# Second cross attention: VectorE copies the values and splits the context between the transposes of the second image's probabilities

## What is computed

```python
q = _split_heads(query @ Wq + bq)
k = _split_heads(key @ Wk + bk)
v = _split_heads(value @ Wv + bv)
score = jnp.einsum('bhqd,bhkd->bhqk', q, k) / scale
score = score + mask * -1000000000.0
attn = jax.nn.softmax(score, axis=-1)
ctx = jnp.einsum('bhqk,bhkd->bhqd', attn, v)
ctx = ctx.transpose(0, 2, 1, 3).reshape(query.shape[0], -1, D)
return ctx @ Wo + bo
```

## Time and profile before

| | us |
|---|---|
| median of 3 runs | 1159.03 |
| lowest and highest | 1158.91, 1160.18 |
| the profiled execution | 1158.4 |
| its span (first to last instruction) | 1157.1 |
| TensorE busy | 1134.1 |
| VectorE busy | 749.6 |
| ScalarE busy | 537.0 |
| GpSimd busy | 244.7 |

### The profile page before, as it was taken

One profiled execution on the slowest core, in us unless ns is written; L12 is line 12 of the kernel. 1 busy time (PEld: TensorE's weight loads), 2 busy tenths in 40 slices (PEclk: granted clock), 3 DMA queues, 4 the chain that ended last, 5 costly groups with the idle time before them and its releaser, 6 DMA issues.

```text
span 1157.1 us, 21749 instructions
## 1 busy us (share of the span) xinstructions
PE 1134.1 (98%) x8729; PEld 845.8 (73%) x8729; DVE 749.6 (65%) x1523; ACT 537.0 (46%) x1036; POOL 244.7 (21%) x308
## 2 busy tenths in 40 slices
PE   7999999999999999999999999999999999999997
PEld 4655488776658777777777777777888678887886
DVE  6367488769894756666566666665797866546632
ACT  3244457653222655656565656555554532223421
POOL 2300013266740432121212222211431100000000
PEclk9999999999999999999999999999999999999999
DMA  9759710100305264444444445444800502224211
GB/s 349 275 216 395 282 51 1 49 35 1 109 19 182 44 139 93 92 92 92 92 92 92 94 91 101 91 102 76 115 13 2 81 3 35 37 38 75 35 37 36
DMA packets 325671, 111.57 MB, mean 96 GB/s; under 512 B 301834, under 2 KB 302908, under 8 KB 321348
## 3 DMA queue, kind: packets, MB, share of 16 engines
q1 hardware_dynamic: 324224, 109.11, 37.3%
q10 hardware_dynamic: 1348, 1.09, 0.3%
HBM read 65.59 MB, written 20.97 MB: 75 GB/s over the span
## 4 chain that ended last, share of the span: by engine, by line
PE 90%; DVE 5%; SPq 2%; DMA 1%; issue 1%; ACT 1%; POOL 0%; DVEq 0%; ACTq 0%
PE bank L303 66%; PE bank L1972 3%; PE bank L583 2%; PE bank L601 2%; PE bank L1988 2%; PE bank L1163 2%; PE bank L259 2%; SPq L1871 2%; PE bank L519 1%; PE bank L1185 1%; PE bank L1130 1%; PE bank L1127 1%; PE bank L1114 1%; PE bank L2445 1%; DVE stats L227 1%
## 5 line engine op out<-in xcount | busy, mean ns | idle before, releaser
L1909 POOL COPY PT<-W 32x512 f32<-32x512 f32 x120 | 84.0, 700 | 308.4 <-DVE W L2122 227.2
L2111 DVE CUSTOM_DVE_ANT_0 W<-bank,W 128x512 f32<-128x512 f32 x128 | 80.8, 687 | 102.0 <-PE bank L1972 98.5
L2202 ACT ACTIVATE K<-bank,vecT 128x512 f32<-128x512 f32 x64 | 43.8, 689 | 164.5 <-PE bank L303 164.5
L2223 ACT ACTIVATE W<-W,low 128x512 f32<-128x512 f32 x128 | 90.7, 711 | 16.9 <-DVE low L2111 16.9
L303 PE MATMUL bank<-xT,wT 128*128 128x512 f32 x384 | 92.6, 390 | 0.8 <-ACT W L3161 0.5
L303 PE MATMUL bank<-Wkv,Wq 128*128 128x512 f32 x384 | 92.7, 396 | 0.0
L303 PE MATMUL bank<-Wkv,ctxT 128*128 128x512 f32 x384 | 92.0, 394 | 0.0
L303 PE MATMUL bank<-ctxT,Wkv 128*128 128x512 f32 x384 | 90.1, 392 | 1.2 <-DVE ctxT L320 1.2
L303 PE MATMUL bank<-Wq,Wkv 128*128 128x512 f32 x384 | 89.8, 390 | 0.0
L303 PE MATMUL bank<-woT,hR 128*128 128x512 f32 x384 | 87.8, 390 | 0.7 <-DVE W_late L3073 0.5
L303 PEld LDWEIGHTS bank<-Wkv,ctxT 128*128 128x128 f32 x384 | 70.8, 188 | 22.2 <-ACT K L2202 5.7
(11 more groups left out here) (377 smaller groups left out, 2119.9 us busy)
## 6 DMA issues: line engine op xcount, KB each, us to landing
PT<-W SPq DMA_DIRECT2D x360, 64.0 KB, 2.1
W<-ctx_turned SPq DMA_DIRECT2D x16, 1024.0 KB, 5.8
W<-in_ctx_dram SPq DMA_DIRECT2D x8, 1024.0 KB, 11.2
ctx_turned<-ctxT SPq DMA_DIRECT2D x8, 1024.0 KB, 8.2
ctx_turned<-W SPq DMA_DIRECT2D x8, 1024.0 KB, 7.1
XT<-in_ctx_dram SPq DMA_DIRECT2D x4, 1024.0 KB, 11.6
XT<-in_L_ffn_wi_dram SPq DMA_DIRECT2D x64, 64.0 KB, 2.1
raw_own<-in_ctx_dram SPq DMA_DIRECT2D x3, 1024.0 KB, 11.1
```

The costliest lines, as they stand in the source:

```text
L1909: pool.tensor_copy(there, here).then_inc(kept_p.s, 1)
L2111: dve.tensor_tensor_reduce(out=PR[:, j, :], in0=bank[:, 4 + j % 4, :], in1=mask, scale=1.0, scalar=3.0e38, op0=ALU.add, op1=ALU.min, accum ...
L2202: act.activation(K[:, m, :], bank[:, n % 4, :], ACT.Identity, bias=pcol("L1_xattn_bk", m)).then_inc(ring_a.s, 1)
L2223: act.activation(PR[:, j, :], PR[:, j, :], ACT.Exp, bias=low[:, j:j + 1], scale=-1.0, accum_out=total[:, j:j + 1]).then_inc(expd.s, 1)
```

## The change

It is in `vector` and for image 1 alone (`i == 1`); the other engines keep their order, and no instruction is added or taken away.

- the copy of values 0 moves up, ahead of score rows 4 to 7;
- of the first four transposes two stay where they were; then come the second reciprocals, the copy of values 1, and the four subtractions that split the context of image 2 (`context_v(2, r)`), and behind them the other two transposes (probabilities 2 and 3);
- the attended product's copy and the transposes of probabilities 4 to 7 follow, with no subtractions between them.

```diff
--- before.py
+++ after.py
@@ -2149,18 +2149,24 @@
                     for t in range(4):
                         scores_v(i, t)
                     recips_v(i, 0)
+                    if i == 1:
+                        value_v(1, 0)
                     for t in range(4, XPAIRS):
                         scores_v(i, t)
                     if i == 0:
                         value_v(0, 0)
                     if more:
-                        for t in range(4):
+                        for t in range(2 if i == 1 else 4):
                             probs_v(i, t)
                         recips_v(i, 1)
-                    if i:
-                        value_v(i, 0)
                     if i == 1:
                         value_v(1, 1)
+                        for r in range(4):
+                            context_v(2, r)
+                        for t in (2, 3):
+                            probs_v(1, t)
+                    elif i:
+                        value_v(i, 0)
                     if i:
                         attended_v(i - 1)
                     if not more:
@@ -2168,7 +2174,7 @@
                     if i != 1:
                         value_v(i, 1)
                     if more:
-                        if i:
+                        if i > 1:
                             for r in range(4):
                                 context_v(i + 1, r)
                         for t in range(4, XPAIRS):
```

## The result

| | before | with the change |
|---|---|---|
| median of 6 runs | 1158.98 us | 1162.47 us |
| lowest and highest | 1158.69, 1160.18 | 1161.95, 1165.36 |
| the profiled execution | 1158.4 | 1162.05 |
| its span | 1157.1 | 1160.8 |

The ratio is 1.0033, with a 95% interval from 1.0023 to 1.0043: **slower by 3.5 us**. I had forecast 1161.2 in a range that ended at 1162.4, and given "within 0.2%" the larger share. The time lies just over the range, and next to the rival that I had priced at 1162.9 and given 0.09, the fall of TensorE's clock.

What follows compares the result with a forecast made beforehand. TensorE, 98% busy, was taken to bound the kernel. Strips delayed 3.16 us put image 1's attended product 2.2 us later, the 1.16 us saved included: 1159.03 became 1161.2 us, range 1159.2 to 1162.4.

Steps and rivals of the forecast that it cites:

- within 0.2%: Outcome class: whole time within about 2.3 us of the kernel before, too little to tell from no change; given 0.57.
- the fall of TensorE's clock: Rival: TensorE's clock falls in the new 3.3 us stop before image 1's attended product, costing 1.7 us; 1162.9, chance 0.09.
- the slack of the strips: Image 1's last copied strip lands about a microsecond before its attended product on TensorE needs it.
- VectorE's steps: Reordered VectorE work on images 1 and 2: subtractions start at 413.24, take 2.50 us; probabilities 2 and 3 end 3.16 later.
- the sum: Last strip lands at 433.92 + 3.16 - 0.21 = 436.87, so image 1's attended product starts at 437.1.
- The first term, +2.2 us at the attended product: Late strips start image 1's attended product at 437.1 instead of 434.89; +2.0 to +2.4 by the first dozen's pace.
- The granted clock stays at 1.00: Sign expected in the changed kernel's profile: no drop of TensorE's clock through its 3.3 us stop.
- The rival's price: Clock fall costs 1.7 us: at the kernel's start 16 transposes took 3.65 us, later 1.91; chance 0.09.
- Nothing absorbs the shift: Behind image 1's attended product both orders match and TensorE is busy almost throughout, so the +2.2 us stays.
- The gain that the change reaches for: TensorE's 1.16 us wait for VectorE's subtractions, ahead of the keys of image 2, goes away.
- wait gone, strips in time: Rival: the 1.16 us wait ahead of image 2's keys goes and the strips are not late; 1157.9, chance 0.08.

Runs made afterwards that it cites:

- load_last: Changed kernel, but for image 1 SyncE issues the load of image 3's context behind the second dozen of strips; 1.0009 against the kernel before, median 1159.95 us.
- the change's second trace: Profile of the unaltered changed kernel, run again beside the follow-up runs; that batch measured 1.0035 against the kernel before, median 1162.86 us.
- ahead_2: Changed kernel with two of the four subtractions moved behind probabilities 2 and 3; 1.0024 against the kernel before, median 1162.93 us.
- swap: Changed kernel, but for image 2 too the values 1 product and its copy go ahead of the previous image's attended product; 1.0014 against the kernel before.
- fill: Changed kernel plus twelve extra, unused TensorE matmuls in the stop before image 1's attended product; 1.0024 against the kernel before, median 1161.64 us; repeated, 1.0033.
- four_first: Changed kernel with all four first transposes ahead of the subtractions; 0.9994 against the kernel before, median 1158.53 us.
- best_near: `four_first` plus one wait holding GpSimd's first-half strip copies of image 1 until the subtractions are done; 0.9993 against the kernel before, median 1158.91 us.
- copy_only: Kernel before with only the copy of values (1,0) moved ahead of score rows 4 to 7 of image 1; 1.0000 against the kernel before.

## Why the prediction was wrong

- **What bounds the kernel, and the slack of the strips.** Right. The queue's twenty-four strips were the next thing late, and moving the load off them gives 2.1 us back (`load_last`).
- **VectorE's steps.** Right in size. Without the 0.21 us the reciprocals came at 412.55 (I said 412.53 to 412.67 with the hand-over), the subtractions took 2.50 us as chosen, not 3.33, and the copy by GpSimd starts behind them. One step was missing: I took the casts by ScalarE to be ready at their old time. With the subtractions moved forward the load of that context is on the path (it landed at 413.09, ScalarE waited 0.39 us for it, VectorE 0.25). Probability 3 was ready 3.5 us later, not 3.16. In the change's second trace this wait isn't there, and the sum holds.
- **The first term, +2.2 us at the attended product.** 2.47 and 2.14 in two traces. Right. The first dozen took 8.14 and 8.01 us, where I had taken the middle of 7.98 and 8.40.
- **The step that failed** is that the sum put the fall of TensorE's clock at nothing: "The granted clock stays at 1.00". It fell in the new stop and cost 1.43 us in the profiled execution and 1.61 in the change's second trace, on top of the +2.2. I had described this as a rival and given it 0.09, because I had one row of a stop that brought the clock down, over 4 us, and read it as if shorter ones did not. It bounds nothing from below: stops of 3.90, 3.58, 3.77 and 2.65 us all did, while 1.56 and 1.36 us did not in their traces. The stop was mis-sized as well, 3.90 and 3.58 us for 3.3, but `ahead_2` shows that 3.3 would not have been short enough either. The page of the Trainium skill that I set against it (TensorE: Matmul & The Clock Gate, Why this matters for your kernels), with its advice to leave no idle gap between bursts of matmuls, was the better guide: the traces agree with it from 2.65 us up, and show no fall at 1.56 us and below. Had I given this rival the larger share, the forecast would have been 1162.9.
- **The rival's price** of 1.7 us is near the 1.4 to 1.6 us that three orders of VectorE lost, but in part by luck. I took it from slower transposes at the kernel's start as if their clock had been low. The view gives a clock of 1.00 for that stretch, and no row shows a lower one; the trace's clock records begin only at about 11.7 us, behind the slower transposes. That the clock made those 1.7 us is not shown.

```profile
9.00:10.00 1.00, 1.00 (x6) 1.00 (x5) 0.69 (x1) 0.73 (x2) 0.00 (x0) 1.00 1.05 406
```

- **Nothing absorbs the shift.** Right in the main: 3.80 us at image 4, 3.4 at image 15 (796.80 less 402.13, against 793.21 less 401.92) and 3.7 at the end. That VectorE's lateness "comes no later than TensorE wants it" was right only because TensorE was as late itself; `swap` shows it.
- **The gain that the change reaches for.** I took 1.16 us, the gap. It was 1.50: besides the gap, TensorE went 0.2 us slower into it, and its keys took 11.17 us for 11.04 behind it. The gain was in my sum only as what the stop swallowed, so this changed nothing there, but the rival "wait gone, strips in time" should have been 1157.5.
- **What stays open.** The change's executions spread from 1161.8 to 1165.8 us, and those of the kernel before beside its second batch from 1157.8 to 1161.5. In the change's second batch the clock over the whole span ran from 0.999 (1161.92 us) to 0.995 (1165.82 us), so in some executions the clock may not fall and in some it may stay low longer. Neither of these two was profiled. The one that was, at 1164.20 us and 0.996, shows a single fall of the usual size, so its 2.15 us over the first profile are not a second fall. Nor is it settled how much of the 1.4 us the matmuls of `fill` give back in the whole.

## What to carry to other kernels

A wait on the bounding engine is worth only as much as the slack of the wait behind it: list, for the same stretch, what lands next and how long before it is wanted (here 0.7 us), and leave a queue of small DMAs and whoever feeds it out of what is delayed. If a change makes TensorE stand for some microseconds, count the clock's fall as part of the price unless a stop of about that length is in the trace with the clock at 1.00 through it and behind it. And look at which engine starts at the same signal: here VectorE's subtractions and GpSimd's copies started together. The order within VectorE brought the keys 0.50 us forward (`four_first`), and keeping the two apart 0.87 us more (`best_near`), though neither shows in the whole time before the load is moved too.

## What the runs showed of the hardware that I had not expected

- The clock of TensorE can fall when TensorE is at work again: in `ahead_2` it stood for 2.65 us, went on at 436.30, and the granted clock left 1.00 only within the stretch from 437. In the four traces with a fall the clock was at 0.50 for 3.4 us, and the matmuls took 1.43, 1.61, 1.59 and 1.56 us longer.
- Four subtractions of 128x512 on VectorE take 2.48 to 2.50 us alone, 3.33 where GpSimd's copies begin 1.4 us ahead of them, 3.68 where these begin 0.8 us ahead (`copy_only`), and 3.77 at 0.4 us (`four_first`).
- A DMA of 1 MB ahead of twelve of 64 KB in one queue cost the last of these 2.1 us, though its own issue takes 0.62: the 24 strips took 18.4 us with it between them and 16.3 without, and the dozen behind it 9.5 us.
- TensorE's stops with nothing that releases them move when a dozen instructions are added far ahead of them (from two, 1.6 to 1.8 us, to three, 2.4 us, in both traces), so an experiment that adds instructions isn't neutral even where their own time is hidden.
